# Two layers of attention and feed-forward on one core: every TensorE step names one of eight PSUM banks, and all engine orders are laid out anew

## The chip, the core and the metric

The kernel runs on one core of a Trainium2 chip. A core has TensorE (matmuls and transposes, writing to PSUM), VectorE, ScalarE and GpSimd, and SyncE, whose queue issues all DMAs here. PSUM has eight banks of 512 float32 words for each of 128 partitions. The metric is the time of the kernel on the device in microseconds (us), as the median of several runs; less is better.

## The reference

x has 8 sequences of 128 rows of 512 numbers, the context ctx has the same shape. Two layers follow each other, each an attention to ctx and a feed-forward part, each with a residual.

```python
x = x + xattn0(layernorm(x), ctx, ctx)     # 32 query heads of 16, 8 key heads, softmax over the keys, Wo
x = x + ffn0(layernorm(x))                 # x @ weight.T + bias, and a LoRA of rank 16 chosen by sequence
x = x + xattn1(layernorm(x), ctx, ctx)     # 16 heads of 32, softmax over axis 0: batch and head
x = x + ffn1(layernorm(x))                 # x @ W_base.T + b, and an update of rank 40, summed over 3 experts
# xattn1: attn = softmax(Q @ K.T / sqrt(32), axis=0); out = (attn @ V), its heads innermost
# ffn1's update: irfft-like transform (a fixed 512 x 512 matrix) of (x @ enc.T) @ (coefs * mask).T
```

Everything is float32. The kernel keeps that precision by splitting each operand in a high part (rounded to fp32r) and a low part (the difference), and by three matmuls, high x high, low x high and high x low (lines 451, 452, 453).

## The kernel before

The work is cut in steps with names such as `ST.2.3`: a kind, and indices. Each of the five engines has a table of steps (`PE_TEXT`, `ACT_TEXT`, `DVE_TEXT`, `POOL_TEXT`, `SP_TEXT`) and executes them in the order of its table; nothing else orders the work but semaphores. A TensorE step fills a place in PSUM, ScalarE or VectorE (or first one, then the other) empties it. The kinds that matter here, b being the sequence, p a pair of sequences:

- XT.layer.b: four transposes of the normalised x (line 610); ScalarE copies the high part (896), VectorE subtracts the low part (1127). The normalisation is LNs (VectorE 1106 and 1108, root on GpSimd 1356) and LNn (ScalarE 885 or VectorE 1112), into one of three buffers `xn`.
- V0.b: keys and values of layer 0, from ctx and the matrix wkv; ScalarE copies K_raw and V (912, 917). K0.p: keys transposed (630), split by 905 and 1132.
- Q0.p.half: queries of layer 0, 24 matmuls; split by ScalarE (928) and VectorE (1138).
- MX.b.r: scores for the row maxima, two matmuls with 64 rows side by side (655) over two banks; VectorE takes maxima (1145). MT.b transposes the maxima (664), ScalarE negates them (936).
- KL.p, QL.b: six DMAs each on SyncE, which lay keys and queries out in KS and QS (523, 537). DM.b: two DMAs (548) that put the negated maxima into a row of QS.
- ST.b.g: scores less the maximum in one matmul pair over two banks (676); ScalarE takes the exponential to PT (943). PV.b.g: times V (687), copied by ScalarE (950). OB, OX: transposes (695, 704) around the division on VectorE; OX is split by 956 and 1127. WO.b: output projection, added to x on VectorE (1162). LT, F0: LoRA and feed-forward of layer 0.
- K1.g, Q1.g, S1.g, SM.g: layer 1, per pair and group of four heads, g to 15. QX.g spreads Q1 by four DMAs (574). S1 are scores (767); VectorE takes minima of the negated scores over the heads (1198), SM adds them (779), ScalarE takes exponentials (1010). ZP on GpSimd sums, FM, FE, FZ, FR, FF form the factors, NM multiplies P1 by them. V1, PV1, OX1 follow, then XT.3 and F1 or FH, the last feed-forward, and OUT.
- W.matrix.chunk on ScalarE (871) and L.matrix.chunk on VectorE or GpSimd split a weight chunk of 256 KB, which LW on SyncE loaded (501) into one of four staging buffers; LC, CT, CL do the same for ctx, LX loads x, LI the identity.

The eight banks are six places: places 0 to 3 are banks 0 to 3, for all steps of one bank; places 4 and 5 are banks 4 and 5, and 6 and 7, for MX, ST and S1, which need two. `PE_TEXT` names the place behind a colon (`ST.2.3:4`). Each place has a semaphore `unit_free`, which the engine that empties it raises. `take` waits for the place before TensorE fills it, `consumed` waits for one step's place to be emptied:

```python
def consumed(eng, step):
    eng.wait_ge(unit_free[UNIT[step]], USE[step] + 1)
def place(step):
    k = UNIT[step]
    return ps[:, k, :] if k < NG else ps[:, 2 * k - NG, :]
def take(eng, step):
    if USE[step]:
        eng.wait_ge(unit_free[UNIT[step]], USE[step])
    return place(step)
```

Ahead of the steps TensorE does two warm-up matmuls on the zeroed V (line 600, four records in the trace), once GpSimd's step SET.1 has written V0.

Of the kernel before, what the change touches and what calls it, by code (L numbers as in the profile page):

```python
# [67 lines left out]
XT.2.6:1 K1.11:0 SM.8:0 K1.10:3 Q1.12:1 Q1.13:2 SM.9:0 Q1.14:3 S1.10:4 S1.11:5 K1.13:1 K1.12:2 SM.10:0 SM.11:0
K1.14:0 Q1.15:3 S1.12:5 S1.13:4 WM:1 K1.15:3 SM.12:0 SM.13:0 V1.6:1 S1.14:5 S1.15:4 WE.0:3 SM.14:0 V1.7:0
SM.15:0 WE.3:2 WE.1:1 WE.2:3 V1.4:1 V1.5:2 V1.2:0 V1.3:3 PV1.6:1 PV1.7:0 V1.0:3 OX1.6:1 OX1.7:2 PV1.4:0 PV1.5:3  # L70
V1.1:1 OX1.4:2 XT.3.6:0 OX1.5:3 PV1.2:1 PV1.3:2 F1.6:0 OX1.2:1 XT.3.7:2 XT.3.4:3 OX1.3:0 PV1.0:1 PV1.1:2 F1.7:0
OX1.1:1 OX1.0:2 XT.3.5:3 F1.4:0 XT.3.2:1 F1.5:2 XT.3.3:0 F1.2:3 XT.3.0:2 F1.3:1 XT.3.1:3 F1.0:2 FH.1.1:1
# [4 lines left out]
LNn.0.0 W.wkv.0 CT.0.0 W.wkv.1 XT.0.1 CT.0.1 W.wq0.0 XT.0.0 W.wq0.1 W.wq0.2 V0.0 W.wq0.3 V0.1 Q0.0.0 K0.0 CT.0.2  # L77
Q0.0.1 W.wo.0 CT.0.3 LNn.0.2 LNn.0.3 XT.0.3 XT.0.2 V0.3 V0.2 LNn.0.4 MT.0 W.wo.1 Q0.1.0 ST.0.3 W.wo.2 K0.1
ST.0.0 XT.0.4 ST.0.2 XT.0.5 ST.0.1 Q0.1.1 MT.1 PV.0.1 CT.0.4 W.wo.3 Q0.2.0 CT.0.5 PV.0.0 ST.1.2 W.la.0 ST.1.1
ST.1.3 W.lb.0 ST.1.0 MT.2 PV.1.1 OX.0 PV.1.0 W.w0.0 V0.4 ST.2.3 CT.0.6 V0.5 W.w0.1 MT.3 Q0.2.1 ST.2.0 XT.0.6  # L80
# [15 lines left out]
LNs.0.0 LNs.0.1 LNn.0.1 L.wkv.0 CL.0.0 XT.0.1 CL.0.1 XT.0.0 C0 L.wq0.1 LNs.0.4 LNs.0.3 K0.0 Q0.0.0 LNs.0.2
CL.0.2 MX.0.1 Q0.0.1 MX.0.0 MX.0.3 MX.0.2 XT.0.3 XT.0.2 LNs.0.6 MX.1.0 MX.1.1 MX.1.3 Q0.1.0 LNs.0.5 K0.1 LNn.0.5
LNs.0.7 LNn.0.6 XT.0.4 MX.1.2 XT.0.5 Q0.1.1 MX.2.1 MX.2.0 L.wo.3 MX.2.3 Q0.2.0 MX.2.2 L.la.0 CL.0.5 OB.0.0
OB.0.1 CL.0.4 LNn.0.7 MX.3.3 SET.3 MX.3.0 OX.0 MX.3.1 OB.1.1 MX.3.2 OB.1.0 L.lb.0 Q0.2.1 XT.0.6 WO.0 LNs.1.0
# [1379 lines left out]
```

## Time and profile before

| | us |
|---|---|
| median of 3 runs (304.91, 306.61, 307.49) | 306.61 |
| span of the profiled execution, first to last instruction | 305.9 |
| TensorE busy in it | 294.3 (96%) |
| VectorE | 232.8 (76%) |
| ScalarE | 161.5 (53%) |
| GpSimd | 147.8 (48%) |

The profiled execution has no time of its own beside its span; the span is 0.7 us under the median. Busy time of matmuls includes their pipelined tails, so a row of 0.28 us may start every 0.12 us. "Idle before" in a timeline row is the engine's idle time ahead of it, with what ended it. SPq rows are DMA issues; when a DMA has landed shows in who waited for it.

### The profile page before, as it was taken

The numbers are of one execution on the slowest core, as the hardware profiler recorded it, in microseconds if no ns is written. First come the engines' busy times: TensorE is split into PE (matmuls) and PEld (weight loads), VectorE is DVE, ScalarE is ACT, GpSimd is POOL, SyncE is SP. The second block draws the span as 40 slices with busy tenths as digits, with TensorE's granted clock in tenths as the row PEclk, the third lists the DMA queues.
The fourth block names the chain that finished last, engine by engine and source line by source line (L and its number), as shares of the span: only waits on it lengthen the run. The fifth ranks groups of instructions, "written<-read, shape, count | busy, mean of one in ns | idle before, by whom it ended". The sixth has DMA issues, their size and how long they took to land.

```text
span 305.9 us, 6265 instructions
## 1 busy us (share of the span) xinstructions
PE 294.3 (96%) x2150; PEld 231.3 (76%) x2150; DVE 232.8 (76%) x375; ACT 161.5 (53%) x277; POOL 147.8 (48%) x192
## 2 busy tenths in 40 slices
PE   5998899899999999999999999999999999999996
PEld 1876756657677467668898898898996767888885
DVE  3699498758895886764677687899788689988762
ACT  4964577396429645963335652565644274364220
POOL 6684620037121231471320078289356969886651
PEclk9999799999999999999999999999999999999999
DMA  7969929939941965004044024343156512000112
GB/s 246 308 197 193 175 75 156 205 87 130 154 116 40 155 94 117 3 2 157 2 133 110 1 70 137 97 120 105 36 138 191 162 57 74 2 0 36 70 71 103
DMA packets 32822, 33.08 MB, mean 108 GB/s; under 512 B 4294, under 2 KB 21958, under 8 KB 32792
## 3 DMA queue, kind: packets, MB, share of 16 engines
q1 hardware_dynamic: 32792, 32.69, 45.5%
q8 instruction: 18, 0.29, 0.4%
q14 instruction: 12, 0.10, 0.1%
HBM read 18.39 MB, written 2.10 MB: 67 GB/s over the span
## 4 chain that ended last, share of the span: by engine, by line
PE 80%; SPq 8%; DMA 6%; ACT 2%; POOL 1%; issue 1%; DVE 1%; ACTq 0%; POOLq 0%
PE ps L451 17%; PE ps L453 16%; PE ps L452 16%; PE ps L610 5%; PE ps L687 4%; PE ps L767 3%; PE ps L676 3%; PE ps L806 2%; SPq L574 2%; PE ps L655 2%; PE ps L695 2%; SPq L537 2%; PE ps L779 2%; DMA QS<-negmax 2%; DMA Q<-Q1d 1%; DMA QS<-Q_h 1%
## 5 line engine op out<-in xcount | busy, mean ns | idle before, releaser
L1356 POOL TENSOR_SCALAR var_eps<-moments 128x1 f32<-128x1 f32 x32 | 8.1, 252 | 76.0 <-DVE moments L1108 75.6
L1145 DVE TENSOR_REDUCE mx<-ps 128x8 f32<-128x1024 f32 x32 | 38.4, 1219 | 6.4 <-PE ps L655 6.1
L943 ACT ACTIVATE PT<-ps 128x1024 f32<-128x1024 f32 x32 | 32.1, 1022 | 15.5 <-PE ps L676 15.2
L451 PE MATMUL ps<-xT_h,slot_h 128*128 128x256 f32 x128 | 37.6, 293 | 0.5 <-POOL slot_l L1345 0.3
L452 PE MATMUL ps<-xT_l,slot_h 128*128 128x256 f32 x128 | 36.6, 286 | 0.0
L453 PE MATMUL ps<-xT_h,slot_l 128*128 128x256 f32 x128 | 36.5, 285 | 0.0
L1345 POOL TENSOR_TENSOR slot_l<-stg,slot_h 128x512 fp32r<-128x512 f32 x19 | 26.4, 1394 | 12.2 <-ACT slot_h L871 12.2
L896 ACT ACTIVATE xT_h<-ps 128x512 fp32r<-128x512 f32 x24 | 14.2, 596 | 25.2 <-PE ps L610 19.8
L1349 POOL TENSOR_TENSOR ctxT_l<-ctx_in,ctxT_h 128x512 fp32r<-128x512 f32 x11 | 14.4, 1309 | 24.9 <-ACT ctxT_h L880 24.8
L451 PEld LDWEIGHTS ps<-xT_h,slot_h 128*128 128x128 f32 x128 | 25.0, 195 | 1.7 <-issue 1.1
L1386 POOL TENSOR_TENSOR zpart<-P 128x512 f32<-128x512 f32 x16 | 22.0, 1376 | 7.1 <-ACT P L1010 5.9
L1106 DVE BATCH_NORM_STATS2 stats<-X 128x6 f32<-128x512 f32 x32 | 21.8, 682 | 4.6 <-DMA X<-in_x 4.5
L452 PEld LDWEIGHTS ps<-xT_l,slot_h 128*128 128x128 f32 x128 | 25.0, 195 | 0.2
L453 PEld LDWEIGHTS ps<-xT_h,slot_l 128*128 128x128 f32 x128 | 24.9, 195 | 0.0
L1162 DVE TENSOR_TENSOR X<-ps,X 128x512 f32<-128x512 f32 x24 | 16.4, 687 | 9.5 <-PE ps L453 4.5
L1127 DVE TENSOR_TENSOR xT_l<-ps,xT_h 128x512 fp32r<-128x512 f32 x24 | 16.4, 685 | 8.6 <-ACT xT_h L896 8.6
L871 ACT ACTIVATE slot_h<-stg 128x512 fp32r<-128x512 f32 x28 | 19.3, 709 | 5.9 <-PE ps L453 2.4
L1198 DVE TENSOR_REDUCE M<-ps 128x128 fp32r<-128x1024 f32 x16 | 19.2, 1215 | 2.3 <-PE ps L767 2.2
L610 PEld LDWEIGHTS ps<-ident,xn 128*128 128x128 f32 x128 | 14.7, 143 | 7.5 <-issue 4.2
L1010 ACT ACTIVATE P<-ps 128x1024 f32<-128x1024 f32 x16 | 16.1, 1025 | 7.7 <-PE ps L779 7.7
L610 PE MATMUL ps<-ident,xn 128*128 128x128 f32 x128 | 20.0, 282 | 0.0
L880 ACT ACTIVATE ctxT_h<-ctx_in 128x512 fp32r<-128x512 f32 x22 | 13.6, 625 | 12.1 <-PE ps L453 5.1
(165 smaller groups left out, 865.3 us busy)
## 6 DMA issues: line engine op xcount, KB each, us to landing
ctx_in<-in_ctx SPq DMA_DIRECT2D x22, 256.0 KB, 3.4
QS<-Q_h SPq DMA_DIRECT2D x32, 128.0 KB, 4.9
Q<-Q1d SPq DMA_DIRECT2D x64, 64.0 KB, 2.1
X<-in_x SPq DMA_DIRECT2D x8, 256.0 KB, 3.9
stg<-in_wq SPq DMA_DIRECT2D x8, 256.0 KB, 3.3
QS<-Q_l SPq DMA_DIRECT2D x16, 128.0 KB, 4.9
out<-XB SPq DMA_DIRECT2D x7, 256.0 KB, 2.0
stg<-in_wo SPq DMA_DIRECT2D x4, 256.0 KB, 5.6
```

The source lines that it names most:

```text
L451: eng.matmul(dst, left[0], right[0], start=start, stop=False)
L452: eng.matmul(dst, left[0], right[1], start=False, stop=False)
L453: return eng.matmul(dst, left[1], right[0], start=False, stop=stop)
L610: last = pe.transpose(dst[:, c * P:(c + 1) * P], xn[:, n % NXN, c * P:(c + 1) * P], ident[:, :])
L871: act.activation(hi, src, ACT.Copy).then_inc(w_hi, 1)
L943: act.activation(PT[:, g2, :], wide(step).rearrange("p k n -> p (k n)"), ACT.Exp, scale=SCALE0).then_inc(free(step), 1)
L1106: dve.bn_stats(stats[:, layer, b, :], X[:, b, :]).then_inc(stat_done, 1)
L1127: dve.tensor_tensor(lo, place(step).rearrange("p (c t) -> p c t", c=C), hi.bitcast(F32), ALU.subtract).then_inc(free(step), 1)
L1145: dve.tensor_reduce(mx[:, b % 2, :].rearrange("p (x r) -> p r x", r=REP)[:, r, :], wide(step).rearrange("p k (g t) -> p (k g) t", g=4), AX ...
L1198: dve.tensor_reduce(M[:, g // C, 1 + g % C, :], wide(step).rearrange("p k (j q) -> p q (k j)", j=JH), AX_X, ALU.max, negate=True).then_inc ...
L1345: pool.tensor_tensor(lo, src, hi.bitcast(F32), ALU.subtract).then_inc(w_lo_pool, 1)
L1386: pool.tensor_tensor(zpart[:, :, :], P1[:, g, 0:JH, :], P1[:, g, JH:T, :], ALU.add).then_inc(z_step, 1)
```

## The change

Each step names its bank, any of the eight; MX, ST and S1 take that bank and the next (in the new table they begin at 0, 2, 4 or 6), and the others any one. Places freed are counted per emptying engine, in `act_freed` and `dve_freed`, and a step waits for the last users of its banks. All five tables are new. What counted steps by their index in layer 1 (`max_ready`, `fac_ready`, `fac_copied`) now counts them by their place in the table. A staging buffer that held `la` is loaded anew only after the second copy of it.

```diff
-XT.0.1:2 XT.0.0:1 V0.0:0 V0.1:2 Q0.0.0:1 K0.0:0 Q0.0.1:3 MX.0.1:4 MX.0.0:5 V0.2:1 MX.0.3:4 XT.0.2:3 MX.0.2:5
+XT.0.1:0 XT.0.0:2 V0.0:7 V0.1:5 Q0.0.0:2 K0.0:0 Q0.0.1:1 MX.0.0:4 V0.2:6 MX.0.2:0 MX.0.3:2 XT.0.3:7 MX.1.3:4 V0.3:1
+MX.0.1:2 XT.0.2:1 MX.1.0:4 MT.0:6 MX.1.2:2 K0.1:0 MX.1.1:6 Q0.1.1:1 ST.0.2:2 ST.0.3:4 Q0.1.0:0 XT.0.5:4 MT.1:5
...
-SET.0 SET.2 SET.1 LNs.0.0 LNs.0.1 L.wkv.1 L.wq0.0 L.wq0.2 L.wq0.3 KM.0 LNs.0.2 LNs.0.3 CL.0.3 KM.1 LNs.0.4
+SET.1 SET.2 SET.0 LNs.0.0 LNs.0.1 L.wkv.1 L.wq0.0 L.wq0.2 L.wq0.3 KM.0 LNs.0.3 KM.1 CL.0.3 LNs.0.5 LNs.0.2 LNs.0.4
...
+WIDE = ("MX", "ST", "S1")
+BANK = {step: bank for step, bank in PE_BANKS if step in FILLS}
+BEFORE, LAST_OF = {}, {}
+for step, bank in BANK.items():
+    mine = (bank, bank + 1) if step[0] in WIDE else (bank,)
+    BEFORE[step] = [LAST_OF[k] for k in mine if k in LAST_OF]
+    LAST_OF.update({k: step for k in mine})
...
         def consumed(eng, step):
 
-            eng.wait_ge(unit_free[UNIT[step]], USE[step] + 1)
...
+            if step in ACT_FREES:
+                eng.wait_ge(act_freed, ACT_FREES[step] + 1)
+            else:
+                eng.wait_ge(dve_freed, DVE_FREES[step] + 1)
 
         def place(step):
-            k = UNIT[step]
-            return ps[:, k, :] if k < NG else ps[:, 2 * k - NG, :]
+            return ps[:, BANK[step], :]
...
         def take(eng, step):
 
-            if USE[step]:
-                eng.wait_ge(unit_free[UNIT[step]], USE[step])
+            by_act = [ACT_FREES[s] for s in BEFORE[step] if s in ACT_FREES]
+            by_dve = [DVE_FREES[s] for s in BEFORE[step] if s not in ACT_FREES]
+            if by_act:
+                eng.wait_ge(act_freed, max(by_act) + 1)
+            if by_dve:
+                eng.wait_ge(dve_freed, max(by_dve) + 1)
             return place(step)
...
                             chunk_split(sp, old)
+                        if old[0] == "la":
+                            sp.wait_ge(la_copied, 1)
```

GpSimd at the start of the program (V and KS are the tiles that are preset); before:

```order
L1318 MEMSET minus_half 128x1
L1325 MEMSET KS 128x2048
L1320 MEMSET V0 128x1024
L1322 MEMSET V0 128x32
L1356 ISA
L1356 TENSOR_SCALAR var_eps<-moments 128x1
```

and after:

```order
L1335 MEMSET V0 128x1024
L1337 MEMSET V0 128x32
L1340 MEMSET KS 128x2048
L1333 MEMSET minus_half 128x1
L1371 ISA
L1371 TENSOR_SCALAR var_eps<-moments 128x1
```

The KS memset now stands behind the two of V, and so behind what TensorE's warm-up waits for.

SyncE from KL.0 (line 523, now 538) to the maxima of sequence 0 (548, now 563) and the DMA behind them; before:

```order
L523 DMA KS<-K_h 16x4x256 x2
L523 DMA KS<-K_l 16x4x256
L523 DMA KS<-K_h 16x4x256 x2
L523 DMA KS<-K_l 16x4x256
L501 DMA stg<-in_wo 128x512
L537 DMA QS<-Q_h 16x4x512
L537 DMA QS<-Q_l 16x4x512
L537 DMA QS<-Q_h 16x4x512 x2
L537 DMA QS<-Q_l 16x4x512
L537 DMA QS<-Q_h 16x4x512
L548 DMA QS<-negmax 1x16x128 x2
L501 DMA stg<-in_wo 128x512
```

and after:

```order
L538 DMA KS<-K_h 16x4x256 x2
L538 DMA KS<-K_l 16x4x256
L538 DMA KS<-K_h 16x4x256 x2
L538 DMA KS<-K_l 16x4x256
L552 DMA QS<-Q_h 16x4x512
L552 DMA QS<-Q_l 16x4x512
L552 DMA QS<-Q_h 16x4x512 x2
L552 DMA QS<-Q_l 16x4x512
L552 DMA QS<-Q_h 16x4x512
L563 DMA QS<-negmax 1x16x128 x2
L488 DMA ctx_in<-in_ctx 128x512 x2
```

The load of a chunk of wo that stood between keys and queries is gone from there (two context loads follow the maxima, where a chunk of wo followed).

ScalarE in the steps of sequences 1 and 2: PT rows are exponentials (ST), OTs is PV's copy, negmax is MT, slot1_h a chunk of wo; before, from ST.1.1 to W.w0.0:

```order
L943 ACTIVATE PT<-ps 128x1024 x2
L871 ACTIVATE lb_h<-stg 128x512
L943 ACTIVATE PT<-ps 128x1024
L936 ACTIVATE negmax<-ps 32x128
L950 ACTIVATE OTs<-ps 128x512
L956 ACTIVATE OT_h<-ps 128x512
L950 ACTIVATE OTs<-ps 128x512
L871 ACTIVATE slot2_h<-stg 128x512
```

and after, from PV.0.0 to OX.0:

```order
L965 ACTIVATE OTs<-ps 128x512
L958 ACTIVATE PT<-ps 128x1024
L943 ACTIVATE Q_h<-ps 128x2x256
L886 ACTIVATE slot1_h<-stg 128x512 x2
L958 ACTIVATE PT<-ps 128x1024
L951 ACTIVATE negmax<-ps 32x128
L958 ACTIVATE PT<-ps 128x1024
L943 ACTIVATE Q_h<-ps 128x2x256
L927 ACTIVATE K_raw<-ps 128x128
L932 ACTIVATE V0<-ps 128x8x16
L971 ACTIVATE OT_h<-ps 128x512
```

Two chunks of wo now stand right ahead of ST.1.0 and of MT.2; before, a chunk of lb and, with two exponentials between, the two copies of la stood there.

## Rows read from the trace of the kernel before

**Rows 1.** The page, parts 1 and 2: busy time; granted clock in tenths.

```profile
PE 294.3 (96%) x2150; PEld 231.3 (76%) x2150; DVE 232.8 (76%) x375; ACT 161.5 (53%) x277; POOL 147.8 (48%) x192
...
PEclk9999799999999999999999999999999999999999
```

**Rows 2.** Waits, TensorE: waited for, us in total, times, longest.

```profile
PE ps L600 <- POOL V L1322: 3.7, 1, 3.7
PE ps L676 <- DMA QS<-negmax: 3.0, 2, 1.7
PE ps L451 <- ACT V L917: 0.7, 1, 0.7
PE ps L767 <- DMA Q<-Q1d: 0.5, 1, 0.5
...
PE ps L451 <- POOL wkv_l L1345: 0.2, 1, 0.2
```

**Rows 3.** Timeline, TensorE, 0 to 13 us: start, us, what, idle before.

```profile
3.71 3.78 PE L600 MATMUL ps<-V 128*128 128x512 f32 x4 [3.71 <-POOL V L1322]
...
7.34 1.35 PE L610 MATMUL ps<-ident,xn 128*128 128x128 f32 x8
...
12.28 0.36 PE L451 MATMUL ps<-xT_h,slot_h 128*128 128x256 f32 x1 [0.34 <-POOL slot_l L1345]
```

**Rows 4.** Timeline, GpSimd, 0 to 14 us.

```profile
0.75 1.80 POOL L1325 MEMSET KS<- 128x2048 f32 x1
2.49 0.95 POOL L1320 MEMSET V<- 128x1024 f32 x1
3.50 0.15 POOL L1322 MEMSET V<- 128x32 f32 x1
```

**Rows 5.** Timeline, TensorE, 28 to 37 us.

```profile
28.87 0.60 PE L610 MATMUL ps<-ident,xn 128*128 128x128 f32 x4
31.19 0.73 PE L676 MATMUL ps<-QS,KS 49*128 49x512 f32 x4 [1.72 <-DMA QS<-negmax]
31.84 0.58 PE L451 MATMUL ps<-xT_h,slot_h 128*128 128x256 f32 x1
...
35.21 0.30 PE L451 MATMUL ps<-xT_h,slot_h 128*128 128x256 f32 x1
...
36.39 0.50 PE L676 MATMUL ps<-QS,KS 49*128 49x512 f32 x2
```

**Rows 6.** Timeline, SyncE's DMA issues, 0 to 44 us.

```profile
20.55 0.58 SPq L501 DMA_DIRECT2D stg<-in_wo  x1
21.23 0.55 SPq L537 DMA_DIRECT2D QS<-Q_h  x1
...
25.11 0.60 SPq L537 DMA_DIRECT2D QS<-Q_h  x1
25.80 1.20 SPq L548 DMA_DIRECT2D QS<-negmax  x2
```

**Rows 7.** Timeline, VectorE, 17 to 27 us.

```profile
19.80 0.68 DVE L1138 TENSOR_TENSOR Q_l<-ps,Q_h 128x512 fp32r<-128x512 f32 x1
20.40 3.48 DVE L1145 TENSOR_REDUCE mx<-ps 128x8 f32<-128x1024 f32 x3
```

**Rows 8.** Timeline, ScalarE, 22 to 50 us.

```profile
25.52 0.25 ACT L936 ACTIVATE negmax<-ps 32x128 fp32r<-32x128 f32 x1
...
27.27 0.63 ACT L871 ACTIVATE slot_h<-stg 128x512 fp32r<-128x512 f32 x1 [1.50 <-DMA stg<-in_wo]
```

**Rows 9.** Timeline, TensorE, 54 to 67 us.

```profile
58.29 0.50 PE L676 MATMUL ps<-QS,KS 49*128 49x512 f32 x2 [1.30 <-DMA QS<-negmax]
...
62.53 0.50 PE L451 MATMUL ps<-slot_h,OT_h 128*128 128x512 f32 x1 [0.66 <-ACT V L917]
```

**Rows 10.** The maxima's DMA (line 548), issue to landing.

```profile
DMA to landing us min/median/max: 1.8/1.9/4.9
```

**Rows 11.** Windows: stretch, busy us (count) of five engines, clock, DMA share, GB/s.

```profile
30.00:36.00 6.00, 4.81 (x26) 4.59 (x27) 3.41 (x8) 2.73 (x4) 2.72 (x4) 0.72 1.07 183
```

More of the change, by code:

```diff
@@ L68 @@
[L68 to L72, printed above, removed]
@@ L74 @@
+F1.2:0 XT.3.0:2 F1.3:1 XT.3.1:0 F1.0:3 FH.1.1:1 FH.1.0:3
 """
 ACT_TEXT = """
[L77 to L80, printed above, removed]
@@ L93 @@
+LNn.3.4 LNn.3.7 XT.3.7 XT.3.4 PV1.0 PV1.1 LNn.3.3 XT.3.5 XT.3.2 XT.3.3 XT.3.0 XT.3.1
 """
 DVE_TEXT = """
[L96 to L99, printed above, removed]
@@ L158 @@
 NMS, NMS_POOL = numbered(DVE_ORDER, "NM"), numbered(POOL_ORDER, "NM")
+MAXIMA, FACTORS = numbered(DVE_ORDER, "S1"), numbered(DVE_ORDER, "FF")
+COPIED = {}
+for step in ACT_ORDER:
+    if step[0] == "FP":
+        for g in range(C * step[1], C * step[1] + C):
+            if ("NM", g) in NMS_POOL:
+                COPIED[g] = len(COPIED) + 1
 SUMS = numbered(POOL_ORDER, "XB")
@@ L304, in build @@
         psum_full = sem("psum_full")
-        unit_free = [sem(f"unit_free{k}") for k in range(NG + 2)]
+        act_freed, dve_freed = sem("act_freed"), sem("dve_freed")
         split_hi = sem("split_hi")
@@ L949, in _ @@
                         filled(act, ("OB", b - 1, gq))
-                    act.activation(OTs[:, gq, :], place(step), ACT.Copy).then_inc(free(step), 1)
+                    act.activation(OTs[:, gq, :], place(step), ACT.Copy).then_inc(act_freed, 1)
                 elif kind == "OX":
@@ L1034, in _ @@
                     act.wait_ge(bv_ready, 1)
-                    act.activation(mt[:, :], place(step), ACT.Copy).then_inc(free(step), 1)
+                    act.activation(mt[:, :], place(step), ACT.Copy).then_inc(act_freed, 1)
                 elif kind == "BV":
@@ L1055, in _ @@
                         all_filled(act, [("S1", GROUPS - 2), ("S1", GROUPS - 1)])
[L1056 removed]
+                    act.activation(O1T[:, n % 2, :], place(step), ACT.Copy).then_inc(act_freed, 1)
         @block.vector
@@ L1097, in _ @@
                     src = stage(key)
-                    dve.tensor_tensor(src, place(step), src, ALU.add).then_inc(free(step), 1)
+                    dve.tensor_tensor(src, place(step), src, ALU.add).then_inc(dve_freed, 1)
                 elif kind == "LNs":
@@ L1161, in _ @@
                     filled(dve, step)
-                    dve.tensor_tensor(X[:, b, :], place(step), X[:, b, :], ALU.add).then_inc(free(step), 1)
+                    dve.tensor_tensor(X[:, b, :], place(step), X[:, b, :], ALU.add).then_inc(dve_freed, 1)
                 elif kind == "LT":
@@ L1180, in _ @@
                             op0=ALU.mult, op1=ALU.add)
-                    last.then_inc(free(step), 1)
+                    last.then_inc(dve_freed, 1)
                 elif kind in ("K1", "Q1"):
@@ L1204, in _ @@
                     low = M[:, (p + 1) % PAIRS, 0, :]
-                    dve.wait_ge(max_ready, C * (p + 1))
+                    dve.wait_ge(max_ready, max(MAXIMA[("S1", C * p + c)] for c in range(C)) + 1)
                     if p:
@@ L1397, in _ @@
                     g = step[1]
-                    pool.wait_ge(fac_copied, sum(s[1] >= g // C * C for s in NMS_POOL))
+                    pool.wait_ge(fac_copied, COPIED[g])
                     pool.tensor_tensor(P1[:, g, :, :], P1[:, g, :, :],
```

177 lines of the change are left out of this document (90 added, 87 removed).

## The prediction

> **What bounds the kernel now.** I read the page's shares first: TensorE is busy 294.3 us of the span, 96% [rows 1]. The matmuls are the same 2150 before and after (the same steps, in another order), so the change can only win back time in which TensorE stands still or runs at its lower clock. Second, the list of what TensorE waited for [rows 2]: 3.7 us before the first matmul, twice a DMA of negated maxima (3.0), once ScalarE's copy of V (0.7), once a DMA of Q (0.5). The third entry is the only one that can be a wait for a PSUM place. Third, the clock line [rows 1]: one slice of forty has a 7; the window 30 to 36 gives 0.72 [rows 11], a stretch at 1.2 GHz instead of 2.4. All of that but the DMA of Q lies before 63 us; there the score phase of layer 0 runs and the sequencer of SyncE is filled with DMA issues of some 0.6 us each [rows 6]. From 63 us on the timeline of TensorE has next to no hole, so a new order has little to win there and something to lose.
>
> How long each step occupies TensorE I take to be unchanged. What a step costs more when it is followed by one on a half array (MX, ST, S1) or by a transpose depends on the neighbours, and I counted these pairs in both orders: 43 against 34 successions of a full-array step or transpose by a half-array step, but 17 against 32 of transpose by transpose. At about 0.2 and 0.1 us each that is -1.8 and +1.5, nothing in sum.
>
> **Start.** GpSimd now zeroes V before KS. The KS memset is 1.80 us [rows 4], so the warm-up matmuls can start at 3.71 - 1.80 = 1.9 us; they take 3.78 [rows 3] and end at 5.7. The first real step, XT.0.1, can't move with them: its input X[1] is now the third load and not the second, one issue (0.6) later, and the identity falls behind too, so it starts at 7.34 + 0.6 = 7.9 instead of 7.34. Before, the warm-up ran straight into the transposes [rows 3]; now 2.2 us of nothing lie between. Rows 5 show what such a gap did: a wait of 1.72 us, and from 31.84 on 15 matmuls in 3.37 us (0.225 each), after 35.21 nine in 1.18 (0.13 each). The low clock cost 15 x 0.095 = 1.4 us. In the Trainium skill, "TensorE: Matmul & The Clock Gate", Part 1, the rule is that the throttled clock is the default and activity releases it; the two stretches here agree with it. I take it that the early warm-up is wasted and the first steps run at 1.2 GHz: 7.9 + 4.4 (the stream from 7.34 to 12.28 without its two waits of 0.2 and 0.34 [rows 2, 3]) + 1.4 = 13.7, less 0.2 that the first transposes lost before as well: Q0.0.0 starts 1.2 us later than its 12.28 [rows 3]. Bounds: -0.3 (the wait of 0.34 gone, since W.wq0.0 now stands ahead of both transposes' copies on ScalarE, and the clock full) and +2.0.
>
> **The first wait for maxima (31.19).** DM.0, which carries the maxima of sequence 0, was issued at 25.80, right behind QL.0 (last issue 25.11 + 0.60), though ScalarE had them from 25.52 + 0.25 [rows 6, 8]. So SyncE's queue and the maxima were equally late. Now LW.wo.1 is gone from between KL.0 and QL.0 (20.55 to 21.23, 0.68 us) and KL.0 itself comes earlier, since both engines serve K0.0 before Q0.0.0. The maxima don't: VectorE takes five row maxima in a row after the Q split, 5 x 1.16 = 5.8 (three took 3.48 [rows 7]), where before one lay ahead of it, and four are needed. Started 1 us earlier (18.8), that ends at 25.2, MT.0 is copied by 25.7, as before. With the start's 1.2 it is 26.9. The landing was slow: the second issue at 26.4, the use at 31.19, 4.7 us; over all DM steps it is 1.8 at least, 1.9 in the median, 4.9 at most [rows 10]. QL.0 has now left SyncE over a microsecond ahead and a 256 KB chunk less is in the queue, so I take 3.0 (nearer to the median), bounds 1.9 and 4.9: 26.9 + 0.6 + 3.0 = 30.5. TensorE gets there, with the same sum of steps ahead, at 28.87 + 0.60 + 1.2 = 30.7 [rows 5]. The wait of 1.72 is gone, and start and wait together give 30.7 - 31.2 = -0.5 us (bounds -2.0 and +1.9).
>
> **The clock after it.** With no gap of 1.7 us at one place the drop at 31.84 should go: -1.4. Bounds -1.6 and 0, for the row maxima still make TensorE wait in pieces between 21 and 27.
>
> **New waits there.** Q0.1.0 goes into bank 0, which VectorE frees with the K0.1 split, now behind two maxima, a normalisation and statistics: +0.5 (0 to 1.2, one maximum). OX.0 goes into the bank of MT.2. ScalarE copies MT.2 only after W.wo.1, W.wo.0 and an exponential, and these two chunks are now issued behind KL.1, at about 41.5. While it waits for a chunk (it did for 1.50 us at 27.27 on the same chunk, issued at 20.55 [rows 6, 8], 6.7 us before) everything behind it on ScalarE stands: the exponential ST.1.0, MT.2, and so DM.2, PV.1.0 and OX.0. With 4 us to landing OX.0 waits 0.6; bounds 0 and 3.0.
>
> **The second pair (58.29, 62.53).** The waits of 1.30 and 0.66 [rows 9] go. DM.2 stood behind six issues of KL.1 and a weight chunk; now KL.1 comes before QL.2, and between MT.2 and its first user stand two V0 steps (24 matmuls, 3.1 us at 0.13), both PV steps and four score steps. WO.0 waited for the bank of V0.5, whose copy stood behind a context load on ScalarE; it now has the bank of OB.1.1. -1.96, bounds -2.0 and -0.5.
>
> **Rest.** S1.8 finds its Q, since Q1.9 and Q1.8 are served in that order and two more steps lie ahead of S1.8: -0.5 (0 to -0.5). Behind 63 us the new places are reused sooner: 32 steps take a bank whose last user ended under 1.5 us of TensorE steps earlier, 19 before. Most of those distances still cover a maximum (1.16) or a copy, so I give 0.3. In the last stage one more operation of 0.68 [rows 7] stands on VectorE before the factors of the second pair, behind which PV1.4 and PV1.2 come: 0.4. Together +0.7, bounds 0 and 1.5. The new counting costs nothing: an engine frees its places in its own order, so waiting for its count is waiting for the same instruction. The added wait of SyncE for la_copied names a copy that is long done.
>
> **Sum.** -0.5 - 1.4 + 0.5 + 0.6 - 1.96 - 0.5 + 0.7 = -2.6 on the profiled span of 305.9: 303.3. The median of the three runs, 306.6, lies 0.7 above that span, so the forecast is 304.0.
>
> **A page that speaks against it.** Bank freedom itself is worth 0.66 us in the rows, the one wait for V's place [rows 9]; the rest of my gain is order. The Trainium skill, "TensorE: Matmul & The Clock Gate", section "HAM oscillation", tells of a kernel in which double-buffering PSUM "gave no further gain". By it the places would give nothing and this sum would lose only those 0.66.
>
> **Rivals.** (1) The clock is full from the first transpose, because the warm-up still counts. Then Q0.0.0 starts 0.3 earlier instead of 1.2 later; DM.0 becomes the limit and gives back part of it: 1.4 us less than the forecast, 302.6. Against it: the 2.2 us gap is longer than the one that cost the clock at 31.84. (2) Nothing in sum: the waits move. The maxima still land after 4.7 us, the clock drops at 32 as well, so -0.5 becomes +0.5 or more and the -1.4 goes; 306.4. For it: SyncE, VectorE and the DMA queue have the same work to do before 60 us. (3) Slower: W.wo.1 on ScalarE. If the chunk takes 6.7 us as at 27.27 [rows 6, 8], it lands at 48.2, ST.1.0 and MT.2 follow at 50.2, and OX.0 waits 3.0 instead of 0.6; a stand of 3 us drops the clock again, 1.4: 304.0 + 2.4 + 1.4 = 307.8. It decides from a landing over some 5 us on. (4) More is won than I count: being 2 to 3 us ahead, layer 0's DMAs are all off the path and small holes under 0.2 us go as well; 301.
>
> **Chances.** Forecast 0.34, (1) 0.2, (2) 0.18, (3) 0.13, (4) 0.15. A measurement of this kernel, whose runs spread from 304.91 to 307.49, tells about 1% from no change. Under 303.5 lie (1), (4) and a little of the forecast: 0.41. Over 309.7 lies (3) joined with (2): 0.10. Within 1%: 0.49. The range takes in (4) and (3): 300.7 to 308.2; the forecast's own is 302.8 to 305.3.
>
> **What would show it.** In the profile after: matmuls of the warm-up from 1.9 us, and the granted clock before 12 us; ST.0.2's wait for the maxima under 0.5 us; no 7 in the clock line near 32 us; no wait over 1 us on L676's counterpart; an idle ScalarE ahead of W.wo.1 near 45 us, with OX.0's transposes behind it; S1.8 without a DMA wait. Wrong would make me: a clock that is low at a second place, a maximum that lands late, or many short waits of TensorE for VectorE between 42 and 60 us.

## The result and the profile after

| | before | after |
|---|---|---|
| median, us (lowest to highest, 11 runs each) | 306.61 (304.41 to 309.11) | 309.42 (306.79 to 311.65) |
| profiled execution: time | - | 309.06 |
| profiled execution: span | 305.9 | 307.3 |

The ratio of after to before is 1.010, 95% interval 1.0066 to 1.0133: the change costs 1%, 2.8 us, where the prediction said 2.6 us less, and 309.42 lies outside its range. TensorE does the same 2150 matmuls, so the loss should stand in its waits and its clock. The ratio leaves out the slowest runs, those over 1.5% above the fastest of their kernel. The page of after, busy time and granted clock (beside [rows 1]):

```profile
PE 291.9 (95%) x2150; PEld 232.3 (76%) x2150; DVE 231.7 (75%) x375; ACT 162.1 (53%) x277; POOL 149.8 (49%) x192
...
PEclk9799999899999999999999999999999999999999
```

What TensorE waited for in after, in the form of [rows 2] (waited for, us in total, times, longest):

```profile
PE ps L625 <- DVE xn L1127: 3.6, 1, 3.6
PE ps L719 <- ACT negmax L951: 2.9, 1, 2.9
PE ps L615 <- POOL V L1337: 1.9, 1, 1.9
PE ps L464 <- POOL ctxT_l L1364: 1.2, 1, 1.2
PE ps L625 <- ACT V L932: 1.1, 1, 1.1
PE ps L464 <- DVE stg L1113: 0.5, 1, 0.5
PE ps L821 <- DVE P L1285: 0.4, 2, 0.2
```

Read against [rows 2]: the three entries behind the first (two DMAs of maxima, V0.5's copy, the DMA of Q) are gone, 3.0 + 0.7 + 0.5 = 4.2 us. In their place stand OX.0 2.9 (L719), K1.8 1.2 (L464, a context half from GpSimd), XT.0.2 1.1 (L625, V0.3's bank) and V1.0 0.5 (the bank of WE.2): 5.7 us. The first wait was 3.7 and is 1.9 + 3.6 now, with the warm-up between its parts. The timeline of TensorE, start:

```profile
1.93 3.58 PE L615 MATMUL ps<-V 128*128 128x512 f32 x4 [1.93 <-POOL V L1337]
9.16 1.94 PE L625 MATMUL ps<-ident,xn 128*128 128x128 f32 x8 [3.65 <-DVE xn L1127]
...
14.15 0.28 PE L464 MATMUL ps<-xT_h,slot_h 128*128 128x256 f32 x1
```

The warm-up starts at 1.9 as foreseen, but XT.0.1 comes at 9.16 (before 7.34, [rows 3]) and Q0.0.0 at 14.15 (12.28). VectorE shows why: X[1], now the third load, is there at 6.21, and its normalisation stands behind GpSimd's root.

```profile
6.21 0.69 DVE L1121 BATCH_NORM_STATS2 stats<-X 128x6 f32<-128x512 f32 x1 [1.19 <-DMA X<-in_x]
...
8.47 0.55 DVE L1127 TENSOR_SCALAR xn<-X,moments,rstd 128x512 f32<-128x512 f32 x1 [0.77 <-POOL rstd L1375]
```

Around OX.0: first TensorE, then ScalarE, then SyncE's issues.

```profile
32.57 0.73 PE L691 MATMUL ps<-QS,KS 49*128 49x512 f32 x4
...
52.69 0.89 PE L719 MATMUL ps<-ident,O 128*128 128x128 f32 x4 [2.85 <-ACT negmax L951]
...
53.59 0.41 PE L465 MATMUL ps<-wkv_l,ctxT_h 128*128 128x256 f32 x1
53.80 0.41 PE L466 MATMUL ps<-wkv_h,ctxT_l 128*128 128x256 f32 x1
```

```profile
37.85 0.25 ACT L951 ACTIVATE negmax<-ps 32x128 fp32r<-32x128 f32 x1
...
48.92 0.63 ACT L886 ACTIVATE slot_h<-stg 128x512 fp32r<-128x512 f32 x1 [2.39 <-DMA stg<-in_wo]
50.95 0.63 ACT L886 ACTIVATE slot_h<-stg 128x512 fp32r<-128x512 f32 x1 [1.39 <-DMA stg<-in_wo]
51.48 1.00 ACT L958 ACTIVATE PT<-ps 128x1024 f32<-128x1024 f32 x1
52.38 0.25 ACT L951 ACTIVATE negmax<-ps 32x128 fp32r<-32x128 f32 x1
```

```profile
34.41 0.61 SPq L552 DMA_DIRECT2D QS<-Q_h  x1
38.13 2.11 SPq L563 DMA_DIRECT2D QS<-negmax  x2
40.34 1.23 SPq L538 DMA_DIRECT2D KS<-K_h  x2
...
44.78 1.07 SPq L516 DMA_DIRECT2D stg<-in_wo  x2
```

The list of waits names "negmax" for OX.0, the copy of MT.2 on ScalarE. That copy takes 0.25 us; the cause is two rows above it. ScalarE stood 2.39 and 1.39 us for the two chunks of wo, with the exponential of ST.1.0 and MT.2 queued behind, and SyncE had issued these chunks only at 44.78. They stand in its order behind DM.1, whose issue waits for MT.1: ScalarE copied it at 37.85, and until 38.13 SyncE had issued nothing for 3.1 us (since 34.41 + 0.61). In the kernel before, the chunks of wo are issued ahead of DM.1. At the top of TensorE's rows ST.0.2 starts at 32.57 with no bracket: the wait of 1.72 in [rows 5] is gone. Between 56 and 66 us no row of TensorE has a bracket: both waits of [rows 9] are gone.

Windows of after (columns as in [rows 11]) show both stretches at 1.2 GHz (clock 0.50), one behind the warm-up and the 3.65 us of standing, one behind OX.0's 2.85:

```profile
8.60:12.00 3.40, 2.84 (x14) 2.87 (x15) 3.40 (x5) 3.28 (x6) 3.04 (x2) 0.50 0.92 290
12.00:50.00 38.00, 36.47 (x277) 28.96 (x276) 30.56 (x49) 22.76 (x41) 15.50 (x22) 1.00 0.67 163
...
53.00:56.40 3.40, 3.40 (x18) 3.18 (x17) 1.29 (x2) 1.25 (x4) 1.15 (x1) 0.50 0.45 116
```

GpSimd ahead of K1.8 (202.59 us on TensorE). CL.1.4, the row of L1364, is queued behind ZP.4, whose last part waits 2.04 us for VectorE's R:

```profile
197.53 1.08 POOL L1404 TENSOR_TENSOR zpart<-zpart 128x256 f32<-128x256 f32 x1
200.65 0.47 POOL L1410 TENSOR_TENSOR ZA<-zpart 128x128 f32<-128x128 f32 x1 [2.04 <-DVE R L1251]
201.07 1.27 POOL L1364 TENSOR_TENSOR ctxT_l<-ctx_in,ctxT_h 128x512 fp32r<-128x512 f32 x1
```

Before, CL.1.4 stood ahead of ZP.4 (with LNs.2.6 between them). A prediction that reads only TensorE's order does not see this exchange on GpSimd, and mine did not.

### The profile page after: what moved, and what is told of

It is laid out like the page before. It is cut to its first block, busy times and chain, and to the rows that moved or that the text cites. A ratio compares the mean times of both kernels' runs of the same rounds, so it can differ in the third digit from the quotient of the medians.

```text
span 307.3 us, 6267 instructions
## 1 busy us (share of the span) xinstructions
PE 291.9 (95%) x2150; PEld 232.3 (76%) x2150; DVE 231.7 (75%) x375; ACT 162.1 (53%) x277; POOL 149.8 (49%) x192
## 4 chain that ended last, share of the span: by engine, by line
PE 69%; DVE 11%; POOL 8%; issue 5%; DMA 4%; ACT 1%; POOLq 1%; DVEq 0%; SPq 0%; ACTq 0%
PE ps L464 14%; PE ps L465 13%; PE ps L466 13%; PE ps L702 5%; PE ps L625 4%; PE ps L782 3%; PE ps L691 3%; PE ps L670 3%; DMA out<-XB 3%; PE ps L710 3%; DVE P L1285 2%; PE ps L821 2%; DMA QS<-Q_l 2%; PE ps L794 2%; POOL rstd L1375 1%
## 5 line engine op out<-in xcount | busy, mean ns | idle before, releaser
L1360 POOL TENSOR_TENSOR slot_l<-stg,slot_h 128x512 fp32r<-128x512 f32 x19 | 25.7, 1359 | 47.6 <-ACT slot_h L886 47.6
L464 PE MATMUL ps<-xT_h,slot_h 128*128 128x256 f32 x128 | 36.8, 287 | 0.0
L465 PE MATMUL ps<-xT_l,slot_h 128*128 128x256 f32 x128 | 35.8, 280 | 0.0
L1371 POOL TENSOR_SCALAR var_eps<-moments 128x1 f32<-128x1 f32 x32 | 8.9, 277 | 50.3 <-DVE moments L1123 49.7
L464 PEld LDWEIGHTS ps<-xT_h,slot_h 128*128 128x128 f32 x128 | 24.2, 189 | 1.9 <-issue 0.9
L465 PEld LDWEIGHTS ps<-xT_l,slot_h 128*128 128x128 f32 x128 | 24.2, 189 | 0.3
L625 PE MATMUL ps<-ident,xn 128*128 128x128 f32 x128 | 19.7, 283 | 4.8 <-DVE xn L1127 3.6
L625 PEld LDWEIGHTS ps<-ident,xn 128*128 128x128 f32 x128 | 15.6, 145 | 7.9 <-DMA ident<-in_eye 5.0
L911 ACT ACTIVATE xT_h<-ps 128x512 fp32r<-128x512 f32 x24 | 13.9, 595 | 13.1 <-PE ps L625 13.0
L1375 POOL TENSOR_TENSOR rstd<-var_eps,minus_half 128x1 f32<-128x1 f32 x32 | 18.7, 585 | 2.7
L464 PE MATMUL ps<-ctxT_h,slot_h 128*128 128x256 f32 x64 | 18.5, 289 | 1.2 <-POOL ctxT_l L1364 1.2
L466 PE MATMUL ps<-ctxT_h,slot_l 128*128 128x256 f32 x64 | 17.8, 278 | 0.0
```

Of the source, the lines that this page charges most:

```text
L464: eng.matmul(dst, left[0], right[0], start=start, stop=False)
L465: eng.matmul(dst, left[0], right[1], start=False, stop=False)
L466: return eng.matmul(dst, left[1], right[0], start=False, stop=stop)
L625: last = pe.transpose(dst[:, c * P:(c + 1) * P], xn[:, n % NXN, c * P:(c + 1) * P], ident[:, :])
L1360: pool.tensor_tensor(lo, src, hi.bitcast(F32), ALU.subtract).then_inc(w_lo_pool, 1)
L1375: root = pool.tensor_tensor(rstd[:, layer, b:b + 1], var_eps[:, layer, b:b + 1], minus_half[:, :], ALU.pow)
```

## The experiments

My theory after the result: the 1% is four places in the new orders (start, wo casts, CL.1.4, late stage), and the scheme of banks and counters is neutral. The rival: the scheme itself costs, by shared counters or more waits. All kernels but the names-only one are the changed kernel with steps exchanged on one or more engines; each edit is shown as old and new text of that engine's order. Kernels of one heading ran on one chip with the kernel before.

### Four places, one at a time

**GpSimd fills V last, as before (a_warm).**

```diff
 GpSimd
-SET.1 SET.2 SET.0
+SET.0 SET.2 SET.1
```

> The changed kernel with one edit: GpSimd zeroes KS before V again, so the warm-up matmuls start at 3.7 us and not at 1.9. If the early warm-up is what lets the clock fall just ahead of the first transposes (at full clock before it, half from about 8.6 us on for 3.4 us in the changed kernel), the low stretch at the start is gone or lies under the warm-up, Q0.0.0 starts near 13 us instead of 14.15, and the time falls by 1 to 1.4 us. If the late loads alone are the cause, the warm-up ends near 7.3 us and TensorE still stands until 9.2: then XT.0.1 starts at 9.2 as before and the time changes by less than 0.5 us.

**First loads and first steps as before (b_loads).**

```diff
 SyncE
-LW.wkv.0 LX.0 LX.1 LC.0.0 LW.wkv.1 LC.0.1 LI LW.wq0.0
+LX.0 LX.1 LC.0.0 LW.wkv.0 LI LW.wkv.1 LC.0.1 LW.wq0.0
 ScalarE
-W.wkv.0 CT.0.0 LNn.0.0 W.wkv.1 CT.0.1 W.wq0.0 XT.0.1
+LNn.0.0 W.wkv.0 CT.0.0 W.wkv.1 XT.0.1 CT.0.1 W.wq0.0
 VectorE
-L.wkv.0 LNn.0.1 CL.0.0 CL.0.1 XT.0.1
+LNn.0.1 L.wkv.0 CL.0.0 XT.0.1 CL.0.1
```

> The changed kernel with the first loads and the first ScalarE and VectorE steps in the order of the kernel before (X[0] and X[1] first, the normalisation of X[1] ahead of the split of wkv); the warm-up stays early. If the late X[1] is the cause of the late start, XT.0.1 comes at 7.3 to 7.6 instead of 9.16 and Q0.0.0 1.5 us earlier than 14.15, and most of it lasts to the end: 1 to 2 us less. If the maxima's path on VectorE and SyncE absorbs it, the wait of OX.0 takes it back and the time changes by less than 0.5 us.

**The wo casts behind four other steps of ScalarE (c_wo).**

```diff
 ScalarE
-W.wo.1 W.wo.0 ST.1.0 MT.2 ST.1.1 Q0.2.1 V0.4 OX.0
+ST.1.0 MT.2 ST.1.1 Q0.2.1 W.wo.1 W.wo.0 V0.4 OX.0
```

> The changed kernel with one edit: on ScalarE W.wo.1 and W.wo.0 stand behind ST.1.0, MT.2, ST.1.1 and Q0.2.1. Rival 3 of the prediction says that ScalarE, waiting for the two chunks, held back MT.2 and with it the bank of OX.0: then OX.0's wait of 2.9 us shrinks under 0.5, the low clock behind it (3.4 us at half, 1.4 to 1.7 us) goes too, and the time falls by 3 to 4.5 us. If the waits of layer 0 only move (SyncE and VectorE being full), OX.0 or ST.2.3 waits elsewhere and the time falls by less than 1.5 us.

**CL.1.4 ahead of ZP.4 (d_cl).**

```diff
 GpSimd
-LNs.2.7 ZP.4 CL.1.4
+LNs.2.7 CL.1.4 ZP.4
```

> The changed kernel with one edit: on GpSimd CL.1.4 stands ahead of ZP.4, as in the kernel before. ZP.4 took 5.4 us there because its last part waits for FR.0, and K1.8 on TensorE waited 1.2 us for CL.1.4. If that wait lasts to the end the time falls by 1.2 us. If the softmax factors of layer 1 at the end set the time instead, K1.8 is early but the factors' chain or PV1.6 gives it back, and the time changes by less than 0.5 us.

Measured, beside a kernel before of 305.58 us:

| | median | ratio to before, 95% interval | span | what TensorE's waits show |
|---|---|---|---|---|
| a_warm | 307.42 | 1.0061 (1.0029 to 1.0092) | 306.0 | warm-up 3.7, XT.0.1 1.1, OX.0 2.3 |
| b_loads | 306.70 | 1.0040 (1.0006 to 1.0075) | 303.8 | XT.0.1 1.6 instead of 3.6, OX.0 2.5 |
| c_wo | 305.89 | 1.0023 (0.9994 to 1.0052) | 305.4 | OX.0 none, ST.2.3 1.5 |
| d_cl | 306.58 | 1.0056 (1.0024 to 1.0088) | 304.9 | K1.8 none, K1.11 0.4 |

The waits that the edits aimed at shrank or went: XT.0.1's in a_warm and b_loads, OX.0's in c_wo, K1.8's in d_cl. Others came. In a_warm V0.2 waited 1.09 us for a context half from VectorE, in d_cl K1.11 waited 0.4, and in c_wo ST.2.3 (row 59.22, from the timeline of TensorE) waited for the DMA of MT.2's maxima, issued at 50.83.

```profile
59.22 0.74 PE L691 MATMUL ps<-QS,KS 49*128 49x512 f32 x4 [1.53 <-DMA QS<-negmax]
```

Its DMA view gives

```profile
DMA to landing us min/median/max: 1.8/2.0/7.7
```

so this landing was far over the median. It is not c_wo's alone: of the five kernels with the casts behind MT.2, four waited at ST.2.3 (1.5 us in c_wo, 0.8 in k_nostart, 1.0 in l_best, 0.3 in i_ln, none in f_four), and none of the others did. So a part of what is gained at OX.0 moves there, as the rival of c_wo had it.

All four ratios are below the 1.010 of the changed kernel, though each kernel keeps three of the four faults. That asked for a control.

### Control, all four, late stage, and the scheme alone

**The changed kernel again (e_ctl).** No edit.

> The changed kernel, unchanged, as a control beside the other three on one chip. Each of the four single edits of its orders came out 0.4 to 0.8% nearer to the kernel before than the changed kernel had (1.0061, 1.0040, 1.0023, 1.0056 against 1.0100), which is more than the waits that two of them took away (1.2 us of 306 is 0.4%). Theory, the edits each gain what they seem to: 1.010 again, some 308.6 us where the kernel before takes 305.6. Rival, part of the first 1.010 was the chip or the hour, and the edits were worth less: 1.005 to 1.007.

**All four edits (f_four).**

> The four edits together (GpSimd fills the tile of the warm-up first; first loads and first steps of ScalarE and VectorE as before; both wo casts behind four other steps of ScalarE; CL.1.4 ahead of ZP.4). Theory, waits of separate places add up: start 1.0 to 1.9 us back, the wait for OX.0 1.3 to 2.9, K1.8 0.6 to 1.2, against the changed kernel some 3.5 to 4.5 us less, which is a ratio to the kernel before of 0.996 to 1.000. Rival, each wait is only handed on to the next one (ST.2.3 waited 1.5 us for a transfer once OX.0 did not wait, K1.11 0.6 us once K1.8 did not): no better than the best single edit, 1.002 to 1.004.

**VectorE's late stage (g_tail).**

```diff
 VectorE
-WE.0 FZ.3 CE FR.3 FF.3 NM.14 FF.1 NM.12 NM.15 FF.2 FF.0 WE.2 NM.11
+WE.0 CE FZ.3 FR.3 FF.3 NM.14 NM.15 FF.1 NM.12 WE.2 FF.2 FF.0 NM.11
```

> The changed kernel with VectorE's steps in the late stage in another order: CE ahead of FZ.3, NM.15 behind NM.14 at once, and WE.2, whose copy frees the bank of V1.0, ahead of FF.2 and FF.0. In the profile of the changed kernel PV1.6 began 0.6 us behind WE.2's end and V1.0 0.5 us later than its operands allowed. Theory, these waits are part of the 1%: both go, 0.7 to 1.1 us less than the changed kernel. Rival, the following steps are late by FF.0 and NM.11 instead: no difference to the control, within 0.3 us.

**Names and counters alone (h_names).** The five texts are those of before; wide place 5 is written as bank 6.

```diff
 TensorE, wide places throughout
-MX.0.0:5
+MX.0.0:6
```

> The mechanism alone: the changed kernel's code, a bank named at each step and two counters of freed places, with the kernel before's five orders and its six places written as banks (narrow 0 to 3, wide at 4 and at 6). Theory, the mechanism costs and gives nothing, all of the 1% is in the orders: 1.000, within 0.3%. Rival, a counter shared by all places makes a step wait for frees of other places and two waits stand in place of one at 1331 matmuls: slower, 1.003 to 1.010.

Measured, beside a kernel before of 305.65 us:

| | median | ratio to before, 95% interval | span |
|---|---|---|---|
| e_ctl | 307.94 | 1.0077 (1.0038 to 1.0116) | 305.2 |
| f_four | 302.74 | 0.9895 (0.9854 to 0.9936) | 300.1 |
| g_tail | 308.89 | 1.0103 (1.0052 to 1.0154) | 309.5 |
| h_names | 305.64 | 1.0001 (0.9968 to 1.0034) | 304.3 |

**h_names settles the scheme:** 1.0001, no cost and no gain. The rival falls; all of the 1% is order.

**The control** lies at 1.0077, between the two expectations, its interval overlapping the first one's. So 0.2% of each single gain above may be the occasion, and a single edit of 0.2% is not shown by its ratio alone; its wait is. Its profiled execution waited 1.9 us for OX.0, that of after 2.85: the size of this wait varies between executions of one kernel.

**The four single edits against their expectations**, by the ratios to the control: a_warm 0.5 us less, b_loads 1.1, c_wo 1.7, d_cl 0.6, each with an interval of about 1 us and on another chip than the control. b_loads came as its theory had it (XT.0.1 at 7.15, Q0.0.0 at 12.88). In a_warm Q0.0.0 came at 12.42, 1.7 us earlier than in after and with the spacing of the full clock, so the early warm-up is what cost the clock at the start. But at XT.0.2 only 0.3 us of that was left (26.75 against 27.09), from 28 to 36 us the clock was low instead (0.79), and the time fell by far less than the 1 to 1.4 expected. c_wo won about half of the 3 to 4.5 us expected of it, d_cl half of its 1.2.

**f_four** is 5.2 us faster than the control (307.94 - 302.74) and 1.05% faster than the kernel before. That is more than the 3.5 to 4.5 us and the ratio of 0.996 to 1.000 that were expected. The rival falls, the gains do add up: against the control the single edits give 0.16 + 0.37 + 0.54 + 0.21 = 1.3%, all four 1.8%; with intervals of 0.3 to 0.4% on each this doesn't show that they are worth more together. (GpSimd fills the tile of the warm-up last here, as in a_warm and before; the expectation has it the wrong way round.) Its waits, and its clock line:

```profile
PE ps L615 <- POOL V L1337: 3.7, 1, 3.7
PE ps L625 <- ACT V L932: 1.2, 1, 1.2
PE ps L464 <- DVE stg L1113: 0.5, 1, 0.5
```

```profile
PEclk9999999999999999999999999999999999999999
```

Waits are not all of it. The pages of h_names (the old orders) and f_four (the new ones without the four faults), both with a clock line of nines:

```profile
PE 292.9 (96%) x2150; PEld 229.6 (75%) x2150; DVE 233.6 (77%) x375; ACT 161.6 (53%) x277; POOL 147.8 (49%) x192
...
PE 290.5 (97%) x2150; PEld 231.0 (77%) x2150; DVE 230.6 (77%) x375; ACT 162.1 (54%) x277; POOL 148.9 (50%) x192
```

For the same 2150 matmuls TensorE is busy 2.4 us less, over half of the 4.2 us between the two spans (304.3 - 300.1). Busy time includes holes that are shorter than a matmul's tail, so it stays open whether such holes went or the steps follow each other more cheaply. What of it is owed to the free choice of banks is open too: no run has the new orders on the old six places.

ScalarE of f_four, to be laid beside the four ScalarE rows of after above. MT.2 is copied at 47.79, and when the casts' turn comes at 49.62 the chunks are there: two in one row and no bracket.

```profile
47.79 0.27 ACT L951 ACTIVATE negmax<-ps 32x128 fp32r<-32x128 f32 x1 [1.75 <-PE ps L679]
48.22 1.03 ACT L958 ACTIVATE PT<-ps 128x1024 f32<-128x1024 f32 x1 [0.17 <-PE ps L691]
49.15 0.59 ACT L943 ACTIVATE Q_h<-ps 128x512 fp32r<-128x512 f32 x1
49.62 1.15 ACT L886 ACTIVATE slot_h<-stg 128x512 fp32r<-128x512 f32 x2
```

**g_tail** gave nothing (0.3% over the control, well inside the intervals), and its own profile says that I had read the wrong row. VectorE and then TensorE:

```profile
261.58 1.21 DVE L1285 TENSOR_TENSOR P<-P,ps 128x1024 f32<-128x1024 f32 x1
262.71 0.68 DVE L1113 TENSOR_TENSOR stg<-ps,stg 128x512 f32<-128x512 f32 x1
```

```profile
262.94 1.95 PE L821 MATMUL ps<-P,V 128*32 128x128 f32 x64 [0.94 <-DVE P L1285]
264.82 0.50 PE L464 MATMUL ps<-slot_h,ctxT_h 128*128 128x512 f32 x1
```

PV1.6 starts 0.15 us behind the end of NM.12 (261.58 + 1.21 = 262.79), not behind NM.15, which I had moved ahead of it. V1.0's wait for WE.2 did go (no bracket at 264.82), and PV1.6 pays 0.94 for it.

### What the start and the wo casts are worth where nothing follows, and one wait more

**LNs.0.2 ahead of LNs.0.5, with the four edits (i_ln).**

```diff
 GpSimd
-LNs.0.5 LNs.0.2 LNs.0.4
+LNs.0.2 LNs.0.5 LNs.0.4
```

> The four edits together, and LNs.0.2 on GpSimd ahead of LNs.0.5. In the kernel with four edits XT.0.2 waited 1.2 us for the bank of V0.3, whose copy on ScalarE stands behind LNn.0.2, and that waits for LNs.0.2 on GpSimd, which ends at 24.27 us behind the 0.9 us of LNs.0.5. Theory: XT.0.2 starts some 0.9 us earlier and nothing else is late there, 301.8 us and a ratio of 0.986 to 0.990. Rival: ST.0.2 or the steps behind it are met by VectorE's queue of MX copies and MT.0 instead, no change to 302.7.

**The four edits without the wo casts (j_nowo).**

> Three of the four edits, without the one on the wo casts: start as before and CL.1.4 ahead of ZP.4, W.wo.1 and W.wo.0 on ScalarE where the changed kernel has them. It prices the step on which the slower rival of the prediction stood. Theory: OX.0 waits 2 to 3 us again, and in some executions a stretch at half clock follows it (1.4 us each), so 2.0 to 3.5 us over the kernel with all four, some 304.7 to 306.2, ratio 0.996 to 1.001. Rival: with a start that is 1.5 us earlier other waits absorb it (the transfers of wo arrive no earlier, so OX.0 waits longer, and the whole gain of the start is lost at OX.0): 306 or more, ratio 1.001 to 1.004.

**The four edits without the start (k_nostart).**

> Two of the four edits, on the wo casts and CL.1.4; the start is the changed kernel's (GpSimd's tile for the warm-up last, X[1] as the third load, XT.0.1 late). It prices the start where nothing behind it waits. Theory: the 1.3 to 1.9 us that XT.0.1 is late are kept to the end, plus a stretch at half clock in the first 15 us in most executions, 1.5 to 3.0 us over the kernel with all four, 304.2 to 305.7, ratio 0.995 to 1.000. Rival: waits for the wo transfers absorb a late start, within 0.5 us of 302.7.

**i_ln with two banks exchanged and a corrected late stage (l_best).**

```diff
 TensorE
-XT.0.2:1 ... MT.0:6
+XT.0.2:6 ... MT.0:1
 VectorE
-WE.0 FZ.3 CE FR.3 FF.3 NM.14 FF.1 NM.12 NM.15 FF.2 FF.0 WE.2 NM.11
+WE.0 CE FZ.3 FR.3 FF.3 NM.14 NM.12 NM.15 WE.2 FF.1 FF.2 FF.0 NM.11
```

> The kernel with LNs.0.2 ahead of LNs.0.5, and besides: banks of XT.0.2 and MT.0 exchanged (6 and 1 in place of 1 and 6, so that XT.0.2 follows V0.2 and not V0.3), and on VectorE in the late stage CE ahead of FZ.3, NM.12 and NM.15 behind NM.14 and then WE.2, ahead of FF.1. The first late order had NM.12 one step too late: PV1.6 began with its end. Theory: 0.1 to 0.3 us from the banks, 0.5 us from V1.0 and 0 to 0.2 from PV1.6, together 0.6 to 1.0 us under the kernel with LNs.0.2 moved, ratio 0.982 to 0.987. Rival: the chain after V1.0 goes through VectorE's NM copies, which are later now, and nothing is gained.

Measured, beside a kernel before of 306.72 us:

| | median | ratio to before, 95% interval | span |
|---|---|---|---|
| i_ln | 302.10 | 0.9878 (0.9823 to 0.9932) | 299.6 |
| j_nowo | 304.95 | 0.9960 (0.9927 to 0.9993) | 303.1 |
| k_nostart | 305.28 | 0.9944 (0.9904 to 0.9984) | 303.7 |
| l_best | 301.14 | 0.9844 (0.9800 to 0.9888) | 299.9 |

j_nowo and k_nostart lie 2.85 and 3.2 us over i_ln by their medians, 2.5 and 2.0 us by their ratios. 0.5 to 0.8 us of that is i_ln's own edit (the spans of f_four and i_ln differ by 0.5, XT.0.2 waited 1.2 in the one and 0.4 in the other). So **the wo casts cost 1.7 to 2.4 us and the start 1.2 to 2.7** in a kernel without other faults; which of the two costs more isn't shown. That each costs something is: the slowest of i_ln's six runs took 303.79, and of the twelve of each of the other two only two or three lie below that. (In k_nostart the tile of the warm-up is filled first, as in after; the expectation says last.) j_nowo's list names the casts directly, and the start's rival (that waits for wo absorb it) falls in a kernel whose casts stand behind MT.2:

```profile
PE ps L719 <- ACT negmax L951: 2.8, 1, 2.8
```

In i_ln XT.0.2's wait fell from 1.2 to 0.4, in l_best, with a bank freed by V0.2, to 0.2 (now for its own operand):

```profile
24.69 0.66 PE L625 MATMUL ps<-ident,xn 128*128 128x128 f32 x4 [0.40 <-ACT V L932]
```

```profile
24.70 0.63 PE L625 MATMUL ps<-ident,xn 128*128 128x128 f32 x4 [0.18 <-ACT xn L900]
```

It starts at the same time to 0.01 us, with Q0.0.0 0.2 us later in l_best (12.53 against 12.30): the other bank was worth 0.2 us there at most. The late order of l_best still has a wait of 0.8 for P and none for WE.2. Whether l_best beats i_ln isn't shown: the intervals overlap and the profiled spans stand the other way round. Both beat the kernel before, by 1.2 and 1.6%.

## Why the prediction was wrong

It was wrong in sign: -2.6 forecast, +2.8 measured, 5.4 apart.

**Bounds of the kernel, and what goes.** Right. The waits for the maxima at 31.19, for those at 58.29, for V0.5's bank and for Q are all gone in after. The scheme costs nothing: right (1.0001). The Trainium skill, "TensorE: Matmul & The Clock Gate", section "HAM oscillation", tells of a kernel in which double-buffering PSUM "gave no further gain". i_ln's and l_best's equal starts of XT.0.2 (24.69 and 24.70) agree with it at one place; h_names does not bear on it, for it keeps the six places.

**What can be won at all.** Wrong, in the change's favour: I held that only waits and low clock could be won back, and put the dearer and cheaper successions of steps at "nothing in sum". TensorE's busy time fell by 2.4 us from h_names to f_four.

**Start, the term +1.2 in Q0.0.0.** Mis-sized. XT.0.1 came at 9.16, not 7.9: I added one issue (0.6) to the old start, but the statistics could begin only when X[1] landed (6.21; in h_names, with the loads of before, the second statistics ran at 4.23), and then stood in GpSimd's and VectorE's queues. Q0.0.0 was at 14.15, 0.7 over the forecast (12.28 + 1.2 = 13.48) and 1.9 over before; in the four profiled executions of e_ctl, c_wo, d_cl and k_nostart, which start alike, it came at 14.8 to 15.4. The half clock behind the wasted warm-up was right, and a_warm shows its cause. The net -0.5 for start and maxima put ST.0.2 at 30.7; it came at 32.57, 1.4 later than the wait of before ended, not 0.5 earlier: the start's 0.7 and XT.0.2's 1.14 below make up most of that difference of 1.9.

**OX.0 behind the wo casts, the term +0.6.** This is the step that failed most: 2.85 measured. The landing was as I took it (issued at 44.78, in ScalarE's hands at 48.92, 4.1 us). The issue time was not: I had it at 41.5, right behind KL.1. But DM.1 ahead of KL.1 had to wait for MT.1, so SyncE issued nothing from 35.02 to 38.13; DM.1's two issues then took 2.11 us where DM.0's took 1.2, KL.1 began only at 40.34, and the load of X[6] follows it. And the second chunk, which I didn't price, came 2.0 us behind the first. c_wo and f_four show the path: with the casts behind MT.2 the wait at OX.0 is gone. It is rival (3)'s mechanism with another cause: late issue rather than slow landing. With the clock drop of rival (3) behind it in the profiled execution (53.00 to 56.40 at 0.50) it made 3.7 us more than the term. In the times of j_nowo against i_ln it is worth 1.7 to 2.4, for the clock doesn't fall in every execution.

**The clock, -1.4.** The drop at 32 us in the profiled execution of before isn't in every execution of it: h_names, with before's orders, has a clock line of nines; and of the runs of the kernel before beside the first four experiments, 11 with a mean clock of 1.00 took 304.9 us on average, 16 with 0.994 took 306.0. And in after the clock fell in other places. The term took one execution's drop for the kernel's.

**The base.** In every experiment's profiled execution the time is 1.7 to 1.9 us above the span (after: 309.06 - 307.3 = 1.76). I set the median 0.7 above a span of 305.9, so that execution of before must have taken some 307.7 (an estimate), 1.1 over the median: a sum that takes its drop away must start from its own time, and ends then at 307.7 - 2.6 = 305.1, not 304.0.

**New waits.** The +0.5 was laid to Q0.1.0 behind VectorE; what came was XT.0.2, 1.14, behind V0.3's copy on ScalarE, which stands behind a normalisation that GpSimd serves late. K1.8's 1.24 was in no term: my "rest behind 63 us" of +0.7 counted banks, and this is a queue of GpSimd. V1.0's 0.50 lies inside that term.

**The account.** The two profiled spans differ by 307.3 - 305.9 = +1.4, forecast was -2.6: 4.0 to explain. The misses are OX.0 2.25, the clock behind it 1.4, K1.8 1.24, XT.0.2 0.64 and the start 0.67, together 6.2. So some 2.2 us were won elsewhere that I hadn't counted. No single row holds them; TensorE's busy time, 294.3 before and 291.9 after in spite of one more stretch at 1.2 GHz, points to it and not to the listed waits. From spans to medians come 1.06 (the base, above) and 0.36 (after's median over its profiled 309.06): 4.0 + 1.4 = 5.4. The gain that I forecast from the orders is there: with the four edits they give 3.2 us (1.05% of 305.65, f_four), against my 2.6. That the two are near is in part luck, since TensorE's lower busy time, which I hadn't counted, has its share in the 3.2.

**The rivals.** (1) and (4) fell with the start; (2), waits that only move, was half right; (3) named the right place, and 307.8 was nearest. It had 0.13. What would have raised it is the look at SyncE's queue that I took only for DM.0.

## What to carry to other kernels

An order of steps is priced on all its queues: for each step that now stands ahead of a wait-free row, find the slowest thing it waits for (here a chunk of weights, whose load stood on SyncE behind an issue that waited for maxima) and who is queued behind it. A good new order with four bad places can measure worse than the old one: mended one by one they looked worth 0.2 to 0.5%, together 1.8%, and the kernel with them beats the one before. Take the base of a sum from the same execution as its rows, and don't sell a clock drop of one execution as the kernel's.
